# Sum of K times V as the diagonal of a float32 matmul, output bias by matmul, unrotated Q straight from PSUM

## What is computed

```python
QKV = jnp.einsum('bsd,ed->bse', X, W_in) + b_in
Q, K, V = jnp.split(QKV, 3, axis=-1)
Q = rope(Q, rot_dim)                       # rot_dim = 128: the first half of the features
K = rope(K, rot_dim)
A = jnp.sum(feature_map(K) * V, axis=-2)   # feature_map(x) = x / max(norm(x), 1e-12); one row of 256
Y = A[:, None, :] * Q
Y = jnp.einsum('bsd,ed->bse', Y, W_out) + b_out
attn = Y + X
x = _layernorm(x + attn)
...
x = _layernorm(x + ffn(x))                 # 8 experts, the two largest gates, gelu
```

## Time and profile before

| | us |
|---|---|
| runs of the kernel before | 152.34, 152.60, 152.65 |
| median | 152.6 |
| span of the profiled execution, first to last instruction | 150.5 |
| TensorE busy in the span | 135.8 (90%) |
| VectorE | 105.7 (70%) |
| ScalarE | 77.3 (51%) |
| GpSimd | 67.6 (45%) |

### The profile page before, as it was taken

The page is one execution under the profiler, slowest core; times in us unless marked ns, Lnnn a source line. Parts: engine busy times, 40 slices in busy tenths (PEclk is TensorE's granted clock), DMA queues, the critical chain, the costliest instruction groups (busy, mean ns, idle before and its releaser), DMA issues.

```text
span 150.5 us, 2427 instructions
## 1 busy us (share of the span) xinstructions
PE 135.8 (90%) x802; PEld 118.9 (79%) x802; DVE 105.7 (70%) x233; ACT 77.3 (51%) x146; POOL 67.6 (45%) x81
## 2 busy tenths in 40 slices
PE   4999979955999899999999999999999999999920
PEld 4778859825987579897898998998998998989910
DVE  0549899996598938899955965745965654638991
ACT  4515966017076894168064264264265265297571
POOL 3004899913999807048306606707507606000310
PEclk9999997555599999999999999999999999999996
DMA  4899940000003130004000400400300000000034
GB/s 133 213 321 419 387 185 4 0 0 0 2 4 121 44 119 0 0 0 139 4 0 0 139 4 2 139 0 0 139 0 0 0 0 0 4 0 0 0 121 158
DMA packets 4698, 10.55 MB, mean 70 GB/s; under 512 B 545, under 2 KB 2641, under 8 KB 4433
## 3 DMA queue, kind: packets, MB, share of 16 engines
q1 hardware_dynamic: 4688, 10.43, 20.1%
HBM read 9.38 MB, written 1.05 MB: 69 GB/s over the span
## 4 chain that ended last, share of the span: by engine, by line
PE 64%; DVE 20%; DMA 5%; ACT 3%; SPq 3%; issue 1%; ACTq 0%; DVEq 0%
PE ps L878 21%; PE ps L879 20%; PE ps L880 20%; DMA wq<-in_w_q_t 5%; DVE z L607 4%; DVE qa L648 2%; DVE kv L588 2%; SPq L257 2%; DVE x L727 2%; DVE z L678 1%; ACT gT_lo L425 1%; DVE stats L849 1%; DVE fT_lo L699 1%; DVE qb L656 1%; DVE acc L752 1%
## 5 line engine op out<-in xcount | busy, mean ns | idle before, releaser
L738 DVE TENSOR_TENSOR gT_lo<-kv,gT_hi 128x512 fp32r<-128x512 f32 x30 | 26.1, 884 | 26.1 <-ACT gT_hi L509 26.0
L352 POOL TENSOR_TENSOR w_hi<-wraw,zero 128x512 fp32r<-128x512 f32 x16 | 18.9, 1181 | 41.2 <-PE ps L880 41.2
L878 PE MATMUL ps<-w_hi,gT_hi 128*128 128x256 f32 x120 | 33.7, 281 | 0.1
L880 PE MATMUL ps<-w_hi,gT_lo 128*128 128x256 f32 x120 | 33.4, 279 | 0.0
L879 PE MATMUL ps<-w_lo,gT_hi 128*128 128x256 f32 x120 | 33.4, 278 | 0.0
L878 PE MATMUL ps<-fT_hi,w_hi 128*128 128x512 f32 x64 | 25.5, 399 | 0.3 <-DVE fT_lo L699 0.3
L879 PE MATMUL ps<-fT_lo,w_hi 128*128 128x512 f32 x64 | 25.4, 396 | 0.0
L880 PE MATMUL ps<-fT_hi,w_lo 128*128 128x512 f32 x64 | 25.3, 395 | 0.0
L507 ACT ACTIVATE kv<-ps,b_now 128x512 f32<-128x512 f32 x16 | 11.0, 690 | 24.7 <-PE ps L880 24.5
L878 PEld LDWEIGHTS ps<-w_hi,gT_hi 128*128 128x128 f32 x120 | 22.7, 189 | 1.1 <-issue 0.4
L752 DVE SCALAR_TENSOR_TENSOR acc<-ps,comb,acc 128x256 f32<-128x256 f32 x53 | 22.6, 475 | 1.0 <-PE ps L880 0.7
(11 more groups left out here) (139 smaller groups left out, 243.1 us busy)
## 6 DMA issues: line engine op xcount, KB each, us to landing
wraw<-in_expert_w SPq DMA_DIRECT2D x8, 512.0 KB, 3.4
xT<-in_x_t SPq DMA_DIRECT2D x4, 256.0 KB, 5.6
acc<-in_x_tok SPq DMA_DIRECT2D x1, 1024.0 KB, 9.5
rT<-in_rope_t SPq DMA_DIRECT2D x1, 1024.0 KB, 10.8
out<-z SPq DMA_DIRECT2D x4, 256.0 KB, 2.2
wkv<-in_w_kv_t SPq DMA_DIRECT2D x2, 256.0 KB, 3.6
rtok<-in_rope_tok SPq DMA_DIRECT2D x1, 512.0 KB, 7.8
brow<-in_b_rows SPq DMA_DIRECT2D x1, 384.0 KB, 6.4
```

The lines of the kernel that those rows point to most:

```text
L352: g.tensor_tensor(w_hi[:, slot, cols], src, zero[:].to_broadcast([P, 2 * D]), ALU.add).then_inc(w_part, 1)
L738: v.tensor_tensor(low, h[:, i, :], raw(high), ALU.subtract).then_inc(g_lo_ok, 1)
L878: nc.tensor.matmul(dst, lh, rh, start=k == 0, stop=False)
L880: last = nc.tensor.matmul(dst, ll, rh, start=False, stop=k == len(terms) - 1)
```

## The change

- K times V: VectorE's eight products go. ScalarE scales V by `krec` for each token (`v_scaled`), and TensorE multiplies K transposed by it in float32, 128 columns wide, for both feature blocks and all tiles, all between the first and the second half of Q. A is the diagonal of the two 128x128 results; VectorE takes it with the identity as a mask and the sum as accumulated output (`diag`, `acol`).
- The rotation of K is dealt out anew: GpSimd the tiles 0 to 5 in pairs, VectorE 6 and 7 together.
- The output bias comes by a matmul of 33 rows of ones with the high and low part of the bias, which opens each PSUM bank of the projection (`out_bias`); GpSimd makes its parts before its rotations, from a small load of its own. The doubling of X moves into `first_sum`. ScalarE's doubling and GpSimd's residual go.
- The unrotated half of Q: ScalarE writes the high part straight from PSUM with the bias, VectorE the low part straight from PSUM (it was GpSimd's); the copy in between goes.
- The instruction lists of ScalarE and VectorE are put in another order: `wo_hi` and `wo_lo` now stand ahead of the second half of Q.

The diff, cut (declarations, semaphore names and comments of shape left out):

```diff
-        POOL_ROTATES = ((0, 2), (2, 3), (4, 6), (6, 7))
-        DVE_ROTATES = (3, 7)
+        POOL_ROTATES = ((0, 2), (2, 4), (4, 6))
+        DVE_ROTATES = (6, 8)
...
-            sp.dma_start(brow[:], b_rows.partition_broadcast(P)).then_inc(l_brow, 16)
+            sp.dma_start(bkv[:], b_rows.partition_broadcast(P)).then_inc(l_brow, 16)
             load_x_t(2)
             load_x_t(3)
+            sp.dma_start(bo[:], b_out).then_inc(l_bo, 16)
             sp.dma_start(rtok[:], rope_tok).then_inc(l_rtok, 16)
             sp.dma_start(wq[:], w_q_t).then_inc(l_wq, 16)
...
+            pool.wait_ge(l_bo, 16)
+            g.tensor_copy(bo_parts[:], bo[:]).then_inc(bo_hi_ok, 1)
+            pool.wait_ge(bo_hi_ok, 1)
+            g.tensor_tensor(bo_parts[OUT_LOW:OUT_LOW + 1, :], bo[OUT_LOW:OUT_LOW + 1, :],
+                            raw(bo_parts[OUT_LOW:OUT_LOW + 1, :]), ALU.subtract).then_inc(bo_ok, 1)
...
-            def residual(t0, t1):
-                pool.wait_ge(res_dbl, t0 // TPH + 1)
-                g.tensor_tensor(acc[:, t0:t1, :], acc[:, t0:t1, :],
-                                bout.unsqueeze(1).to_broadcast([P, t1 - t0, D]), ALU.add).then_inc(res_ok, 1)
...
-            def q_pass_low(n):
-                pool.wait_ge(q_hi_ok, (1, 3)[n])
-                g.tensor_tensor(gT_lo[:, 1, half(n)], qT[:, 1, half(n)], raw(gT_hi[:, 1, half(n)]),
-                                ALU.subtract).then_inc(q_pass_lo_ok, 1)
             other(0)
-            q_pass_low(0)
-            pool.wait_ge(q_pass_lo_ok, 1)
             other(1)
-            pool.wait_ge(l_brow, 16)
-            residual(0, TPH)
-            q_pass_low(1)
             pool.wait_ge(q_hi_ok, 4)
-            g.tensor_tensor(gT_lo[:, 0, half(1)], qT[:, 0, half(1)], raw(gT_hi[:, 0, half(1)]),
+            g.tensor_tensor(gT_lo[:, 0, half(1)], qT[:, half(1)], raw(gT_hi[:, 0, half(1)]),
                             ALU.subtract).then_inc(q_rot_lo1_ok, 1)
-            residual(4, 6)
-            residual(6, 8)
...
-                if t in (3, 5):
-                    if t == 3:
-                        act.wait_ge(l_x, 16)
-                    four = slice((t - 3) // 2 * TPH, ((t - 3) // 2 + 1) * TPH)
-                    a.mul(acc[:, four, :], acc[:, four, :], 2.0).then_inc(res_dbl, 1)
+            def k_norm(n):
+                act.wait_ge(ksq_ok, (n + 1) * TPH)
+                q4 = slice(n * TPH, (n + 1) * TPH)
+                a.activation(knorm[:, q4], ksq[:, q4], ACT.Sqrt).then_inc(knorm_ok, 1)
+            def v_scaled(t):
+                act.wait_ge(krec_ok, t // TPH + 1)
+                a.activation(z[:, t, :], kv[:, t, D:2 * D], ACT.Copy, scale=krec[:, t:t + 1]).then_inc(vs_ok, 1)
+            for t in range(TPH):
+                k_square(t)
+            k_norm(0)
+            k_square(4)
+            k_square(5)
+            v_scaled(0)
+            v_scaled(1)
+            k_square(6)
+            v_scaled(2)
+            v_scaled(3)
+            k_square(7)
+            k_norm(1)
...
             def q_pass(n):
                 act.wait_ge(q_mm, 2 * n + 2)
-                a.activation(qT[:, 1, half(n)], ps[:, Q_BANK[n][1], :], ACT.Identity,
-                             bias=bq[:, 1:2]).then_inc(q_pass_ok, 1)
-                act.wait_ge(q_pass_ok, n + 1)
-                a.copy(gT_hi[:, 1, half(n)], qT[:, 1, half(n)]).then_inc(q_hi_ok, 1)
+                a.activation(gT_hi[:, 1, half(n)], ps[:, Q_BANK[n][1], :], ACT.Identity,
+                             bias=bq[:, 1:2]).then_inc(q_hi_ok, 1)
             def q_rot_high(n):
                 act.wait_ge(q_rot_ok, n + 1)
-                a.copy(gT_hi[:, 0, half(n)], qT[:, 0, half(n)]).then_inc(q_hi_ok, 1)
+                a.copy(gT_hi[:, 0, half(n)], qT[:, half(n)]).then_inc(q_hi_ok, 1)
             q_raw(0)
+            for t in range(TPH, T):
+                v_scaled(t)
             q_pass(0)
+            q_rot_high(0)
+            act.wait_ge(l_wout, 16)
+            for k in range(KD):
+                act.wait_ge(acol_ok, k + 1)
+                a.activation(wo_hi[:, k, :], wout[:, k, :], ACT.Copy, scale=acol[:, k:k + 1]).then_inc(wo_hi_ok, 1)
             q_raw(1)
-            q_rot_high(0)
-            act.wait_ge(l_wout, 16)
-            act.wait_ge(acol_ok, 1)
-            for k in range(KD):
-                a.activation(wo_hi[:, k, :], wout[:, k, :], ACT.Copy, scale=acol[:, k:k + 1]).then_inc(wo_hi_ok, 1)
             q_pass(1)
...
-            def kv_product(t):
-                if t in DVE_ROTATES:
-                    dve.wait_ge(vrot_ok, DVE_ROTATES.index(t) + 1)
-                else:
-                    dve.wait_ge(rot_ok, [t < t1 for _, t1 in POOL_ROTATES].index(True) + 1)
-                v.tensor_tensor(z[:, t, :], kv[:, t, 0:D], kv[:, t, D:2 * D], ALU.mult).then_inc(kv_prod, 1)
...
             kv_out(3)
-            dve.wait_ge(l_rtok, 16)
-            rotate(3)
             kv_out(4)
             dve.wait_ge(wq_hi_ok, 1)
             v.tensor_tensor(wq_lo[:], wq[:], raw(wq_hi[:]), ALU.subtract).then_inc(wq_lo_ok, 1)
-            kv_product(0)
             kv_out(5)
-            kv_product(1)
-            kv_product(2)
+            k_reciprocal(0)
             kv_out(6)
-            kv_product(3)
-            k_reciprocal(0)
             kv_out(7)
-            rotate(7)
+            dve.wait_ge(kv_ok, T)
+            rotate(*DVE_ROTATES)
             k_reciprocal(1)
-            for t in range(4, T):
-                kv_product(t)
...
-                if n == 1:
-                    dve.wait_ge(q_hi_ok, 2)
-                    v.tensor_tensor(gT_lo[:, 0, half(0)], qT[:, 0, half(0)], raw(gT_hi[:, 0, half(0)]),
-                                    ALU.subtract).then_inc(q_rot_lo0_ok, 1)
-                    dve.wait_ge(a_mm, 1)
-                    v.tensor_copy(acol[:], ps[:, 2:4, 0]).then_inc(acol_ok, 1)
...
+            def q_pass_low(n):
+                dve.wait_ge(q_hi_ok, (1, 3)[n])
+                v.scalar_tensor_tensor(out=gT_lo[:, 1, half(n)], in0=ps[:, Q_BANK[n][1], :], scalar=bq[:, 1:2],
+                                       in1=raw(gT_hi[:, 1, half(n)]), op0=ALU.add,
+                                       op1=ALU.subtract).then_inc(q_pass_lo_ok, 1)
...
             q_products(0)
             q_rotate(0)
-            q_products(1)
+            dve.wait_ge(a_mm, 1)
             for k in range(KD):
+                v.scalar_tensor_tensor(out=diag[:, k, :], in0=ps[:, 2 + k, 0:P], scalar=1.0, in1=ident[:],
+                                       op0=ALU.mult, op1=ALU.mult, accum_out=acol[:, k:k + 1]).then_inc(acol_ok, 1)
+            q_pass_low(0)
+            dve.wait_ge(q_hi_ok, 2)
+            v.tensor_tensor(gT_lo[:, 0, half(0)], qT[:, half(0)], raw(gT_hi[:, 0, half(0)]),
+                            ALU.subtract).then_inc(q_rot_lo0_ok, 1)
+            for k in range(KD):
+                dve.wait_ge(acol_ok, k + 1)
                 dve.wait_ge(wo_hi_ok, k + 1)
                 v.scalar_tensor_tensor(out=wo_lo[:, k, :], in0=wout[:, k, :], scalar=acol[:, k:k + 1],
                                        in1=raw(wo_hi[:, k, :]), op0=ALU.mult,
                                        op1=ALU.subtract).then_inc(wo_lo_ok, 1)
+            q_products(1)
+            q_pass_low(1)
             q_rotate(1)
...
-                    v.tensor_tensor(z[:, t, :], ps[:, 4 + t % 4, 0:D], acc[:, t, :], ALU.add).then_inc(z_ok, 1)
+                    v.scalar_tensor_tensor(out=z[:, t, :], in0=acc[:, t, :], scalar=2.0, in1=ps[:, 4 + t % 4, 0:D],
+                                           op0=ALU.mult, op1=ALU.add).then_inc(z_ok, 1)
...
-            def feature_sum(n):
-                pe.wait_ge(krec_ok, n + 1)
-                for t in range(n * TPH, (n + 1) * TPH):
-                    pe.wait_ge(kv_prod, t + 1)
-                    for k in range(KD):
-                        last = nc.tensor.matmul(ps[:, 2 + k, 0:1], z[:, t, tile(k)], krec[:, t:t + 1],
-                                                start=t == 0, stop=t == T - 1)
+            def feature_sum(t):
+                pe.wait_ge(vs_ok, t + 1)
+                if t < DVE_ROTATES[0]:
+                    pe.wait_ge(rot_ok, t // 2 + 1)
+                else:
+                    pe.wait_ge(vrot_ok, 1)
+                for k in range(KD):
+                    last = nc.tensor.matmul(ps[:, 2 + k, 0:P], kv[:, t, tile(k)], z[:, t, tile(k)],
+                                            start=t == 0, stop=t == T - 1)
                 return last
             pe.wait_ge(wq_lo_ok, 1)
             q_block(0, 0)
             q_block(0, 1)
             pe.wait_ge(kv_ok, T)
-            feature_sum(0)
+            for t in range(T):
+                last = feature_sum(t)
+            last.then_inc(a_mm, 1)
             q_block(1, 0)
-            feature_sum(1).then_inc(a_mm, 1)
             q_block(1, 1)
...
+            def out_bias(t):
```

(10 more changed lines are left out.)

78 lines of the change are left out of this document (40 added, 38 removed).

## The result

The changed kernel takes **147.5 us** (median of 146.63, 147.18, 147.84 and 151.06), the kernel before 152.47 beside it; the ratio is 0.968, with a 95% interval of 0.964 to 0.973. The profiled execution took 146.63 us with a span of 144.8, 5.7 less than before.

A forecast was written before the change was run, and what follows sets the result against it. Before 51.51 us it took VectorE's products, slowed beside GpSimd, as the bound, after it TensorE's experts. Steps reached the experts 7.0 us earlier, loads 0: span 143.5, plus 2.1 outside it, 145.6 us; range 144.3 to 147.9.

The forecast's parts named there:

- rival A: Clock falls to half in TensorE's gap after projection tile 3, losing 1.1 to 2.3 us: 146.7 to 147.9; chance 0.20.
- main case: Whole kernel, clock full: 7.0 us gained, 145.6 us, own range 144.4 to 146.5; chance 0.62.
- Step 1: ScalarE to first half of raw Q, doublings replaced by scaled V copies: raw Q at 21.4, last `kv_out` near 19.1.
- Step 2: VectorE to the second reciprocal, with a collision with GpSimd's `qb`: 23.0, or 21.8 without it.
- Step 3: TensorE's float32 sums: 128 columns at 0.12 us a half, like one column; last out at 25.6, against 29.34.
- Step 4: VectorE to `wo_lo`: diagonals at 0.45 us, one collision of 1.3; projection starts at 29.7, 5.9 us earlier.
- Step 5: VectorE's second half of Q done at 32.1; TensorE's 1.5 us wait for GpSimd's low part counted as covered.
- Step 6: First `z` to the experts: 14.1 us less 1.6 of waits at half clock; 44.5, 7.0 us earlier.
- Step 7: Loads, one more small DMA and a shorter broadcast row: `wq` a little earlier to 0.6 us later, taken as 0.
- Rival B: Clock falls where it fell before, at the sums; whole gain only 4.7 to 5.8 us: 146.8 to 147.9; chance 0.13.
- C: Slower: clock falls at the gap and stays low past 53; until 58 it gives 154.8 us; 0.03 together with D.
- D: Float32 sums each dearer by over 0.4 us than their row, so the edit does not shorten; 0.03 together with C.

The follow-up runs named there:

- the pause filled: Changed kernel plus nine unused 128x128 float32 identity matmuls on TensorE ahead of the projection's fifth tile; 145.69 us, ratio 0.955.
- the long row: Changed kernel with the early broadcast row of 384 KB of the kernel before, its last third not used; 146.28 us, ratio 0.958.
- the sum alone: Changed kernel with output bias and unrotated half of Q both as before, leaving only the new sum of K times V; 149.61 us, ratio 0.985.
- the short row: Kernel before with only the K/V bias (256 KB) in the early broadcast row, the output bias loaded later by itself; 151.33 us, ratio 0.994.

## Why the prediction was right in its range and wrong in its main case

The time, 147.5 us, lies inside 144.3 to 147.9 and inside rival A's 146.7 to 147.9; the main case's own range ended at 146.5. By its steps:

- *Step 1 (raw Q at 21.4, `kv_out` near 19.1).* 20.3 and 18.9. From the end of the root to raw Q ScalarE took 4.1 us for the 3.5 worked out, with 0.3 of it a wait for VectorE's `kv`; with the pause filled it took 3.4. Its start was 1.7 us earlier, which is step 7.
- *Step 2 (23.0).* The second reciprocal was done at 22.3. The collision with GpSimd's `qb` took place, one instruction earlier than I put it, and cost about 1.1 us.
- *Step 3 (0.12 per half, last out at 25.6).* 0.12, and 24.9. 128 columns cost as much as one. The four passes of the Trainium skill (FP8 and Floating Point Precision, TensorE Precision Notes) would have made it 1.9 us more by the prediction's estimate. No run here shows that.
- *Step 4 (0.45 per diagonal, projection at 29.7).* A diagonal takes 0.21 from start to start with a read of 0.08 beside the next: I had doubled it. (The terms of this step also add up to 28.7, not to the 28.4 that I wrote.) The second collision came behind `wo_lo` and not ahead of it: its 1.1 us moved to the other side of the projection's start. The projection started at 28.27, 1.4 us better than forecast, and TensorE's work, forecast as hidden, had no slack left: the four bias matmuls took 0.66 us there.
- *Step 5 (second half at 32.1, a wait of 1.5 us, "so that wait is covered").* **This is the step that failed.** VectorE was at its first `z` by 31.20 and TensorE waited 2.00 us; VectorE did have work meanwhile. But the wait was not free: the clock fell behind it, the next matmuls came 0.21 us apart in place of 0.12, and tile 4 to the gate took 12.08 us where it takes 10.72 to 10.74 with the clock kept.
- *Step 6 (44.5; "these waits go if the clock is full").* The condition did not hold. Its sum puts the gate 12.5 us behind the first `z`; the change took 14.3, and 12.9 with the pause filled (first `z` at 30.67) as with the long row, where the clock held (31.80). So of the 1.7 us too few, 1.36 are the clock's, within the 1.1 to 2.3 that rival A named, and 0.4 are not explained by it. The same step gave GpSimd's lost additions no price; with additions, doublings and broadcast back the kernel is 2.2 us longer by the ratios.
- *Step 7 (loads taken as 0).* `wq` came 2 us earlier in this profile and 0.9 to 1.7 in the others with its loads, outside the bounds I gave it. Little of that reached the end: ScalarE's second four copies wait 1.97 us for VectorE's reciprocal.
- *Rival B* did not come: wide columns kept the clock through the sums. With one column, which is what it rested on, the clock fell in the sums and the Q blocks ran at half speed. *C and D* have nothing in the traces. (C's own sum does not close: half a us for each one from 53 to 58 is 2.5, not 2.2; no chance hung on it.)

The miss of 1.9 us (147.5 for 145.6) is thus a sum of opposite errors, and that it stayed so small is in part luck. The way to the projection was forecast 1.4 us too long. The way from it to the gate was 2.4 too short (17.2 for 14.8): 0.7 of that lies ahead of tile 4, where the moved collision stands, 1.36 are the clock's, 0.3 the rest. What follows was 0.3 too short. The last 0.6 is no error in the kernel: outside the span lie 1.8 us and not the 2.1 that I took from a median and another execution's span, and the profiled execution was 0.9 us below the median.

Rival A at 0.20 and the main case at 0.62 were in the wrong order. Four of the five profiles with a pause of 1.35 to 2.19 us at this place and no fillers lost the clock, one kept it; the two with 4.61 and 4.90 us lost it too. The Trainium skill (TensorE: Matmul & The Clock Gate, section on the second failure mode) spoke for A, with a clock that oscillates through short idles between groups of matmuls. Here it was one fall behind one pause.

## What to carry to other kernels

A wait of TensorE that every other engine has work beside is not thereby free: ask what its clock does. Cheap matmuls in the pause kept the clock here, where shortening the pause did not. To price such a dip, compare from a point right ahead of it (tile 4) and not from the start of the kernel: the gate alone said 1.9 us where 1.36 were the clock's. And cost an edit that takes GpSimd's two-operand work away by what VectorE does in those microseconds. Single effects measured by undoing one part need not sum to the change, and intervals of half a per cent are too wide to tell whether they do.

## What was not expected of the hardware

- The same pause gives different clocks: 1.94 us kept it in one profile; 1.35, 1.89, 2.00 and 2.19 lost it in others, from near 33.5 (pause from 30.67) to near 35.2 (pause from 31.56). Behind the pause of 1.35 us the clock fell only after 2.3 us of unbroken work. A pause of 1.07 us between the sums, in the kernel with the sum alone, kept it.
- The clock's rise at the start varies too. By the spacing of the 512-column matmuls (0.43 us, then 0.23) nine profiles are at full speed from the first K/V matmul (6.3 to 7.1 us) and three from 7.4 to 7.9. That of before with the short row rises only near 11.3 and that of the one-column sums near 11.8, and these two start their last K/V matmul at 19.7 and 20.0, where the others, but for the one with the long row, start it at 17.2 to 17.9. The times of the kernel before spread over 151.2 to 153.1; whether this is the cause stays open.
- With one column, float32 sums let the clock fall in a place where 128 columns, at the same time per matmul, kept it; one profile against nine.
